# The order of GpSimd's additions and of one VectorE subtraction in an eight-element decoder kernel

## The chip, the cores and the metric

The kernel runs on one core of a Trainium2 chip. The metric is the time of one execution on the device, in microseconds. A core has five engines with a queue each, worked off in order: TensorE (PE in the profile; PEld is its weight load), VectorE (DVE), ScalarE (ACT), GpSimd (POOL) and SyncE (SP, which issues the DMAs). They meet only through semaphores.

## The reference, cut to what matters

Two decoder layers over `x` (8 elements of 256 tokens, 128 features) and a context (8 x 512 x 128). The change lies in layer 0, in the stretch where local self-attention of one element runs beside the cross-attention of the element before it:

```python
x = _layernorm(x + _L0_attn_ref(x, ...))          # 16 heads of 8, causal, window 64, relative bias
x = _layernorm(x + _L0_xattn_ref(x, ctx_1024, ...))
# cross-attention: lat = layer_norm(x)*g+b, ctx = layer_norm(context)*g+b
#   q = lat @ Wq;  k, v = split(ctx @ Wkv);  k = apply_rope(k, cos, sin)      16 heads of 64
#   attn = softmax(clip(q k^T / 8, -11, 11));  out = (attn @ v) @ Wo + bo
x = _layernorm(x + _L0_ffn_ref(x, ...))
x = _layernorm(x + _L1_attn_ref(x, ...))          # a scan of 256 steps
x = _layernorm(x + _L1_xattn_ref(x, ctx_1024, ctx_1024, ...))   # linear attention: relu features
x = _layernorm(x + _L1_ffn_ref(x, ...))
```

## The kernel before, in words

The first 50 us prepare weights and the first element. Then comes a loop over the eight elements `b`, and in it over eight **pairs** of heads `p` of the cross-attention (`batch` on each engine). Behind it follow the scan over 256 steps and the last products (from about 822 us on).

*One pair.* TensorE makes the scores in two halves, the units 0 and 1 (L2133; it waits for `kr_ready`, the rotated keys, and for the exponentials of the unit before). ScalarE takes the exponentials of a unit (L1007, `exps`). VectorE clamps them (L1471, `clamp`), which gives four key blocks `prob[.., 0..3, ..]` of 128 x 512. GpSimd adds the four blocks for the softmax's denominator: first to second (L731, behind the first clamp), plus the third (L733, behind the second clamp), plus the fourth (L735, "the last addition", which signals `psum_ready`). One pair later TensorE multiplies the probabilities by the values (L2057, `values_of`) and the added blocks by ones (L2065, `sum_of`, the column sums, which wait for `psum_ready`). VectorE takes the reciprocal (L1373) and multiplies (L1374, `on`). Keys two pairs ahead are prepared beside this: TensorE's split products (L1758 to L1760, "keys a" and "keys b"), VectorE's multiplications by cosine and sine (L1315, L1317), GpSimd's addition of the two (L641, `rotate`, signals `kr_ready`).

*The slots.* The self-attention of element b+1, with the norms and the layer-1 keys and values of its context, is cut into 48 slots, six to a pair, and each engine calls `self_attention(b + 1, 6 * p + i, ..)` at fixed places among the work of the pair. The order on each engine is written out by hand; there is no planner. The last element has no such slots. Slots named below:
- `S_CTX` = 3 (pair 0): VectorE takes the statistics of the context `cb` (L1176, L1179), GpSimd makes scale and bias of them (`scale_and_bias`, L633 to L636). ScalarE applies them at slot 5 (`apply_norm`, L843).
- `S_CN` = 7 (pair 1): TensorE transposes the normed context; ScalarE copies it with gain and bias twice, as `cn_raw` in full precision (L835) and as `cn_s[.., 0, ..]`, the high part (L906); VectorE subtracts the two into `cn_s[.., 1, ..]`, the low part (L1305, signals `cn_split`). The split products need both. `cn_raw` shares its memory with `ctx_t`, which ScalarE writes in slot 14 behind `cn_split`.
- `S_SCORE` = 6, 8, 10, 12, ...: TensorE makes self-attention scores (L1774), VectorE adds the bias and takes row maxima (L1251, L1253); the next scores go to the same two banks, and wait for that.
- `S_AFFINE` = 36, 38 (pair 6): GpSimd multiplies the layer-1 keys by a gain and adds a bias (L678). VectorE's ReLU of them is slot 40 (L1264), and TensorE's product for them slot 44.
- `S_X1` = 37 (pair 6): GpSimd's norm factor (L624, L626) and an addition.

At pair 0 of elements 1 to 7 TensorE also makes the output product of the element before (`output`, L2040; it waits for `on` of pair 7). VectorE adds it (L1380), takes statistics, waits for GpSimd's factor (L624, L626, behind the rotation in its queue), and normalizes (L1190).

Where GpSimd's additions stand among its slots (L726 to L742): slots 0 and 1 come first, then L731 and L733, then slots 2 and 3, then L735, then slot 4, the rotation, at pair 0 the output's factor, then slot 5. Only two slots with work for GpSimd lie at 2 or 3 of a pair: `S_CTX` in pair 0 and the second of `S_AFFINE` in pair 6. VectorE's order in a pair (L1482 to L1499): keys a, first clamp, slots 0 and 1, reciprocal and product of the pair before, second clamp, slot 2, keys b, slots 3 and 4, the output, slot 5.

Of the kernel before, what the change touches and what calls it, by code (L numbers as in the profile page):

```python
# [57 lines left out]
PER_PAIR = 6  # L58
SLOTS = PER_PAIR * PAIRS
S_X, S_K, S_Q, S_CTX, S_V = range(5)  # L60
S_CN = 7
S_MASKED = (3, 4, 5, 6)
S_SCORE = (6, 8, 10, 12, 14, 16, 18, 20)
S_EXP = (range(10, 14), range(14, 19), range(19, 24), range(24, 29))
# [93 lines left out]
def n(b, per, k):  # L158

    return b * per + k  # L160


class Chain:
# [5 lines left out]
    def link(self, instruction):  # L169
        self.k += 1  # L170
        instruction.then_inc(self.sem, 1)
        self.eng.wait_ge(self.sem, self.k)
# [7 lines left out]
def decoder(nc, a, out):  # L180
    with ExitStack() as ctx:
# [412 lines left out]
        def _(pool):  # L594
# [25 lines left out]
            def rstd_of(before, k, count, eps, half=0, ready=var_ready, done=rstd_ready):  # L620

                tiles = slice(4 * half, 4 * half + count)
                pool.wait_ge(ready, before + k + 1)
                link(g.tensor_tensor(var_eps[:, tiles], mv[:, tiles, 1],  # L624
                                     epsilons[:, EPSILONS.index(eps), tiles], ALU.add))
                g.tensor_tensor(rstd[:, tiles], var_eps[:, tiles], minus_half[:, tiles],  # L626
                                ALU.pow).then_inc(done, 1)
# [10 lines left out]
            def rotate(key):  # L638

                pool.wait_ge(p_free["dve"], KEYS_DONE[key])  # L640
                g.tensor_tensor(kr[:, key % 2, :], k_cos[:, :], k_sin[:, :], ALU.add).then_inc(kr_ready, 1)  # L641
# [72 lines left out]
            def rstd_of_f(b):  # L714
                rstd_of(0, b, QT, 1e-3, half=1, ready=f_var, done=f_rstd)

            def batch(b, last=False):

                for p in range(PAIRS):
                    pair = n(b, PAIRS, p)  # L720

                    def slots(lo, hi):
                        for i in range(lo, hi if not last else lo):
                            self_attention(b + 1, PER_PAIR * p + i, SELF_NORMS * (b + 1))

                    slots(0, 2)  # L726
                    pool.wait_ge(clamped, 2 * pair + 1)
                    if pair >= 2:
                        pool.wait_ge(o_full, pair - 1)
                    pp = prob[:, p % 2]  # L730
                    link(g.tensor_tensor(psum[:, p % 2, :], pp[:, 0, :], pp[:, 1, :], ALU.add))  # L731
                    pool.wait_ge(clamped, 2 * pair + 2)
                    link(g.tensor_tensor(psum[:, p % 2, :], psum[:, p % 2, :], pp[:, 2, :], ALU.add))  # L733
                    slots(2, 4)
                    g.tensor_tensor(psum[:, p % 2, :], psum[:, p % 2, :], pp[:, 3, :],  # L735
                                    ALU.add).then_inc(psum_ready, 1)
                    slots(4, 5)
                    if p + 2 < PAIRS or not last:
                        rotate(pair + 2)
                    if p == 0 and b >= 1:  # L740
                        rstd_of(b - 1, 0, QT, EPS_LN, ready=y_var_ready, done=y_rstd_ready)
                    slots(5, 6)  # L742
                    if last and p < B - 1:
                        rstd_of_f(p)

            for b in range(0, B - 1):
                batch(b)
            batch(B - 1, last=True)
            g.tensor_copy(ident16[:, :], ident[:, :]).then_inc(ident16_ready, 1)
            pool.wait_ge(p_free["dve"], ALL_JOBS["dve"])  # L750
# [75 lines left out]
        def _(act):  # L826
# [45 lines left out]
            def self_attention(b, slot, norms):  # L872
# [26 lines left out]
                if slot == S_LAT:  # L899
                    by_feature = dict(scale=cols[:, LAT_G:LAT_G + 1], bias=cols[:, LAT_B:LAT_B + 1])  # L900
                    evacuate(b, A_LAT, lat_raw[:, :], bank_a[:, 0:T], free=False, **by_feature)
                    s.activation(lat_s[:, b % 2, 0, :], bank_a[:, 0:T], ACT.Identity, **by_feature).then_inc(a_free, 1)
                if slot == S_CN:
                    by_feature = dict(scale=cols[:, CTX_G:CTX_G + 1], bias=cols[:, CTX_B:CTX_B + 1])
# [222 lines left out]
        def _(dve):  # L1127
# [97 lines left out]
            def self_attention(b, slot, norms):  # L1225
# [69 lines left out]
                if slot == S_LAT:  # L1295
                    dve.wait_ge(a_free, n(b, ACT_JOBS, SETUP_A + A_LAT + 1) if b >= 1 else FIRST_LAT)
                    w.tensor_tensor(lat_s[:, b % 2, 1, :], lat_raw[:, :], lat_s[:, b % 2, 0, :].bitcast(F32),
                                    ALU.subtract).then_inc(lat_split, 1)
                if slot == S_CN:
                    if b == 0:  # L1300
                        dve.wait_ge(cn_kept, 1)
                    else:
                        dve.wait_ge(a_free, n(b, ACT_JOBS, SETUP_A + A_CN + 1))
                    raw = cn_raw if b >= 1 else cn_raw_first
                    w.tensor_tensor(cn_s[:, b % 2, 1, :], raw[:, :], cn_s[:, b % 2, 0, :].bitcast(F32),  # L1305
                                    ALU.subtract).then_inc(cn_split, 1)
# [12 lines left out]
            def odd_turn(at):  # L1319
                dve.wait_ge(odd_full, at // 2 + 1)  # L1320
                w.tensor_copy(pt[:, 1, :], ob[:, :]).then_inc(odd_free, 1)

            def first_score(at):
                if at % 2 == 0:
                    dve.wait_ge(bias_in[at // 2], 16)
                self_attention(0, S_SCORE[at], 0)
# [4 lines left out]
            for slot in (S_CTX, S_Q, S_V):  # L1331
                self_attention(0, slot, 0)
# [11 lines left out]
            odd_turn(3)  # L1344
            measure_kv(0, 1)
            odd_turn(5)
            self_attention(0, S_CN, 0)
            odd_turn(7)
            odd_turn(9)
            invert_sums(0)  # L1350
# [398 lines left out]
        def _(pe):  # L1749
# [52 lines left out]
            def self_attention(b, slot):  # L1802
                def a_job(job):
                    pe.wait_ge(a_free, n(b, ACT_JOBS, SETUP_A + job))
# [85 lines left out]
                if slot == S_LAT:  # L1890
# [4 lines left out]
                    last.then_inc(a_full, 1)  # L1895
                if slot == S_CN:
                    a_job(A_CN)
# [557 lines left out]
```

## Time and profile before

| | us |
|---|---|
| median of 3 runs | 1050.55 |
| the three runs | 1050.55, 1050.72, 1046.6 |
| the profiled execution, its own time | 1047.62 |
| its span, first to last instruction | 1045.9 |
| TensorE busy | 919.8 (88%) |
| VectorE busy | 681.3 (65%) |
| GpSimd busy | 510.7 (49%) |
| ScalarE busy | 509.6 (49%) |
| mean granted clock of TensorE, share of full speed | 0.944 |

In the rows further down a timeline gives for each instruction (or group of the same) its start in us from the start of the span, its duration in us, engine, line, operation, output and inputs with partitions x elements, and how many; in brackets how long the engine had been idle before, and which engine's work ended that idle time. An instruction's bracket is missing where the engine was not idle. Starts can lie up to 0.1 us ahead of the end of the instruction before, since an engine overlaps the two. A row of the chain gives start, duration and what the chain passed through. A clock of 1.00 is 2.4 GHz, and the low level is 1.2 GHz.

### The profile page before, as it was taken

Reading aid. Unit: us, or ns where it says so; the run is one execution under the profiler, and the core shown is the slowest. Engines: PE = TensorE matmul, PEld = TensorE weight load, DVE = VectorE, ACT = ScalarE, POOL = GpSimd, SP = SyncE. Lnnn points to the kernel's source line nnn. Section 1 sums busy time; section 2 is a strip of 40 time slices with the busy share of each in tenths; the row PEclk is TensorE's granted clock in tenths of the full one; section 3 lists DMA queues with packets and bytes.
Section 4 is the critical chain, followed back from the end, with each engine's and each line's share of the span. In section 5 each row is a group of like instructions: output and inputs, shape, how many; then the busy total and the mean of one; then the engine's idle time right before and its main releaser. Section 6 shows DMA issues by size and latency. Waiting matters only on the chain.

```text
span 1045.9 us, 22097 instructions
## 1 busy us (share of the span) xinstructions
PE 919.8 (88%) x8504; PEld 652.6 (62%) x8504; DVE 681.3 (65%) x1906; ACT 509.6 (49%) x1441; POOL 510.7 (49%) x642
## 2 busy tenths in 40 slices
PE   6689989998999999899989999998988499999922
PEld 4456656666665756566666666666656379888721
DVE  6446577568757766776687577667689543444477
ACT  6655645653663556456636645564233023333324
POOL 2643475356546534654565466446657112333363
PEclk9989999999999989999999999999999589999955
DMA  7000000000000000000000000000000001222211
GB/s 194 21 6 12 1 2 6 12 1 7 11 1 1 7 11 2 1 6 11 2 6 7 6 1 1 1 1 1 21 1 1 0 7 30 32 33 30 33 13 41
DMA packets 60470, 15.09 MB, mean 14 GB/s; under 512 B 41278, under 2 KB 59726, under 8 KB 60238
## 3 DMA queue, kind: packets, MB, share of 16 engines
q1 hardware_dynamic: 60366, 13.69, 6.1%
q8 instruction: 68, 1.11, 0.4%
q14 instruction: 36, 0.29, 0.1%
HBM read 10.51 MB, written 3.17 MB: 13 GB/s over the span
## 4 chain that ended last, share of the span: by engine, by line
PE 64%; DVE 19%; ACT 7%; POOL 5%; issue 3%; DMA 1%; SPq 0%; POOLq 0%; DVEq 0%; ACTq 0%
PE score_banks L2133 10%; PE out_bank L2057 8%; PE score_banks L1758 5%; DVE o_rec L1373 5%; PE bank_a L1753 5%; PE score_banks L2071 4%; DVE prob L1471 3%; PE score_banks L1789 3%; PE score_banks L1760 3%; PE score_banks L1759 3%; PE score_banks L2261 3%; PE bank_d L1774 3%; PE out_bank L2040 2%; PE out_bank L2065 2%; PE bank_d L2274 2%
## 5 line engine op out<-in xcount | busy, mean ns | idle before, releaser
L1007 ACT ACTIVATE prob<-score_banks 128x1024 f32<-128x1024 f32 x128 | 131.0, 1024 | 165.8 <-PE score_banks L2133 165.5
L733 POOL TENSOR_TENSOR psum<-psum,prob 128x512 f32<-128x512 f32 x64 | 81.6, 1275 | 153.9 <-DVE prob L1471 153.9
L2133 PE MATMUL score_banks<-qh,kr 64*128 64x256 f32 x1024 | 150.9, 415 | 2.1 <-ACT qh L916 1.3
L731 POOL TENSOR_TENSOR psum<-prob 128x512 f32<-128x512 f32 x64 | 82.6, 1290 | 98.4 <-DVE prob L1471 98.3
L1373 DVE RECIPROCAL o_rec<-out_bank 128x256 f32<-128x256 f32 x64 | 111.9, 1748 | 26.1 <-PE out_bank L2065 26.0
L2057 PE MATMUL out_bank<-prob,v 128*64 128x256 f32 x1024 | 124.7, 386 | 1.4 <-DVE on L1374 1.4
L2133 PEld LDWEIGHTS score_banks<-qh,kr 64*128 64x128 f32 x1024 | 91.9, 193 | 40.7 <-issue 30.5
L867 ACT ACTIVATE prob<-prob,neg_max 128x128 f32<-128x128 f32 (+1 forms) x256 | 107.1, 426 | 13.5 <-DVE neg_max L1258 13.5
L1471 DVE TENSOR_SCALAR prob<-prob 128x1024 f32<-128x1024 f32 x128 | 101.4, 792 | 12.9 <-ACT prob L1007 12.9
L2057 PEld LDWEIGHTS out_bank<-prob,v 128*64 128x64 f32 x1024 | 67.9, 136 | 46.6 <-issue 17.2
L1056 ACT ACTIVATE prob<-score_banks 128x8 f32<-128x8 f32 x255 | 45.1, 177 | 96.1 <-PE score_banks L2261 96.1
L1315 DVE TENSOR_TENSOR k_cos<-score_banks,cos_t 128x512 f32<-128x512 f32 x56 | 38.2, 682 | 72.4 <-PE score_banks L1760 46.2
L641 POOL TENSOR_TENSOR kr<-k_cos,k_sin 128x512 f32<-128x512 f32 x64 | 82.8, 1294 | 4.4 <-DVE k_sin L1317 3.6
L735 POOL TENSOR_TENSOR psum<-psum,prob 128x512 f32<-128x512 f32 x64 | 81.6, 1275 | 3.9
L2261 PE MATMUL score_banks<-prob,pt 128*64 128x8 f32 x1020 | 74.3, 210 | 0.6 <-ACT prob L1053 0.3
L835 ACT ACTIVATE pt<-bank_a 128x512 f32<-128x512 f32 x84 | 50.2, 598 | 35.5 <-PE bank_a L1753 34.6
L1774 PE MATMUL bank_d<-km,q 64*128 64x128 f32 x480 | 50.6, 330 | 17.9 <-DVE row_max L1253 16.6
L2261 PEld LDWEIGHTS score_banks<-prob,pt 128*64 128x64 f32 x1020 | 53.4, 137 | 20.8 <-ACT prob L1056 14.5
L2071 PE MATMUL score_banks<-w_qkv_t,ident 128*64 128x96 f32 (+1 forms) x336 | 64.8, 277 | 0.0
L1753 PE MATMUL bank_a<-ident,prob 128*128 128x128 f32 x360 | 57.0, 281 | 4.0 <-ACT pt L835 2.3
L1789 PE MATMUL score_banks<-pt,vm 128*32 128x128 f32 x768 | 54.0, 281 | 4.5 <-ACT pt L938 3.8
L760 POOL TENSOR_TENSOR var_eps<-mv,epsilons 128x1 f32<-128x1 f32 x49 | 9.5, 194 | 96.1 <-DVE mv L1575 96.1
(414 smaller groups left out, 2129.8 us busy)
## 6 DMA issues: line engine op xcount, KB each, us to landing
cb<-in_ctx_dram SPq DMA_DIRECT2D x8, 256.0 KB, 2.8
bias_mask<-bias_scratch SPq DMA_DIRECT2D x4, 384.0 KB, 5.4
xb<-in_x_dram SPq DMA_DIRECT2D x8, 128.0 KB, 2.1
prob<-in_L_xattn_Wkv_dram SPq DMA_DIRECT2D x1, 1024.0 KB, 8.4
x_scratch<-v SPq DMA_DIRECT2D x16, 64.0 KB, 1.5
bias_mask<-x_scratch SPq DMA_DIRECT2D x16, 64.0 KB
att_scratch<-on SPq DMA_DIRECT2D x16, 64.0 KB, 1.5
prob<-att_scratch SPq DMA_DIRECT2D x16, 64.0 KB, 3.0
```

The costliest lines, as they stand in the source:

```text
L641: g.tensor_tensor(kr[:, key % 2, :], k_cos[:, :], k_sin[:, :], ALU.add).then_inc(kr_ready, 1)
L731: link(g.tensor_tensor(psum[:, p % 2, :], pp[:, 0, :], pp[:, 1, :], ALU.add))
L867: last = s.activation(pr, pr, ACT.Exp, bias=neg_max[:, qt, j, g:g + 1], accum_out=row_sum[:, qt, j, g:g + 1])
L1007: s.activation(prob[:, p % 2, 2 * u:2 * u + 2, :].rearrange("p k (h q) -> p h k q", h=2), sc[:, 0:2, :].rearrange("p h (k q) -> p h k q", ...
L1373: link(w.reciprocal(o_rec[:, :], bank[:, T:2 * T]))
L1471: w.tensor_scalar(pr, pr, float(np.exp(-CLIP)), float(np.exp(CLIP)), ALU.max, ALU.min).then_inc(clamped, 1)
L1753: return nc.tensor.transpose(out_ap, in_ap, ident[0:in_ap.shape[0], 0:in_ap.shape[0]])
L1789: last = mm(o0_bank[32 * g:32 * g + 32, qt * P:(qt + 1) * P], vm[:, kt, j, 32 * g:32 * g + 32], pt[:, t % 2, i * P:(i + 1) * P], start=(j ...
L2057: mm(o[DH * h:DH * (h + 1), 0:T], v[:, (q // 2) % 2, kb, lo:lo + DH], prob[:, q % 2, kb, T * h:T * (h + 1)], start=(kb == 0), stop=(kb == ...
L2071: mm(bank[0:HALF_ROWS, 0:columns], ident[:, 0:HALF_ROWS], w_qkv_t[:, 0:columns], start=True, stop=True, skip_group_check=True)
L2133: last = mm(sc[:, h, k * T:(k + 1) * T], kr[rows_of, p % 2, kb * P:(kb + 1) * P], qh[rows_of, p % 2, :], start=True, stop=True, skip_group ...
L2261: last = mm(cf[lo:lo + HALF_ROWS, t * B:(t + 1) * B], a_t[:, lo:lo + HALF_ROWS], hid[:, (t - 1) * B:t * B], start=False, stop=True, skip_g ...
```

## The change

The slot of VectorE's low part gets a number of its own, 11 instead of 7: it moves from pair 1's slot 1 (ahead of the reciprocal of pair 0) to pair 1's slot 5 (behind the self-attention scores of slots 8 and 10). TensorE's and ScalarE's part of `S_CN` stays at 7. On GpSimd the slots 2 and 3 of a pair go behind the last addition; with slot 4 they make one call. The call for element 0 follows the new name and stays where it is.

```diff
-S_CN = 7
+S_CN, S_CN_LOW = 7, 11
...
                     link(g.tensor_tensor(psum[:, p % 2, :], psum[:, p % 2, :], pp[:, 2, :], ALU.add))
-                    slots(2, 4)
                     g.tensor_tensor(psum[:, p % 2, :], psum[:, p % 2, :], pp[:, 3, :],
                                     ALU.add).then_inc(psum_ready, 1)
-                    slots(4, 5)
+                    slots(2, 5)
                     if p + 2 < PAIRS or not last:
                         rotate(pair + 2)
...
-                if slot == S_CN:
+                if slot == S_CN_LOW:
                     if b == 0:
                         dve.wait_ge(cn_kept, 1)
...
-            self_attention(0, S_CN, 0)
+            self_attention(0, S_CN_LOW, 0)
```

## Rows read from the trace of the kernel before

**Rows 1.** The page's first part: busy us, share of the span, instructions.
```profile
PE 919.8 (88%) x8504; PEld 652.6 (62%) x8504; DVE 681.3 (65%) x1906; ACT 509.6 (49%) x1441; POOL 510.7 (49%) x642
```
**Rows 2.** Waits of TensorE, 60 to 825 us: total, times, longest.
```profile
PE out_bank L2065 <- POOL psum L735: 16.7, 7, 2.4
PE bank_d L1774 <- DVE row_max L1253: 14.8, 7, 2.4
```
**Rows 3.** The chain of waits, in two stretches.
```profile
243.80 0.65 PE out_bank L2065 x4
...
269.05 0.03 DVE cn_s L1305
```
**Rows 4.** Windows between low parts: us, PE busy, granted clock, DMA share, GB/s.
```profile
172.54:269.05 96.51, 90.75 (x691) 0.98 0.02 5
269.05:364.23 95.18, 89.27 (x691) 1.00 0.02 5
```
**Rows 5.** Timeline of GpSimd, pair 6 of element 1.
```profile
241.27 1.26 POOL L678 TENSOR_TENSOR k<-k,l_b 128x512 f32<-128x512 f32 x1
242.49 1.26 POOL L735 TENSOR_TENSOR psum<-psum,prob 128x512 f32<-128x512 f32 x1
243.71 1.45 POOL L641 TENSOR_TENSOR kr<-k_cos,k_sin 128x512 f32<-128x512 f32 x1
```
**Rows 6.** Timeline of VectorE, pairs 6, 7 and 0.
```profile
242.56 1.47 DVE L1264 TENSOR_SCALAR k<-k 128x512 f32<-128x512 f32 x1 [0.69 <-POOL k L678]
245.26 0.69 DVE L1315 TENSOR_TENSOR k_cos<-score_banks,cos_t 128x512 f32<-128x512 f32 x1 [1.23 <-POOL kr L641]
...
256.72 0.42 DVE L1374 TENSOR_TENSOR on<-out_bank,o_rec 128x256 f32<-128x256 f32 x1
```
**Rows 7.** Timeline of TensorE, the output product in pair 0 of element 2.
```profile
258.18 3.74 PE L2040 MATMUL out_bank<-wo,on 128*128 128x128 f32 x32
```
**Rows 8.** Timeline of GpSimd, pair 0 of element 2.
```profile
258.17 1.27 POOL L733 TENSOR_TENSOR psum<-psum,prob 128x512 f32<-128x512 f32 x1 [1.80 <-DVE prob L1471]
260.29 0.20 POOL L633 TENSOR_TENSOR var_eps<-mv,epsilons 128x4 f32<-128x4 f32 x1 [0.85 <-DVE mv L1179]
...
262.09 1.27 POOL L735 TENSOR_TENSOR psum<-psum,prob 128x512 f32<-128x512 f32 x1
...
264.83 0.71 POOL L626 TENSOR_TENSOR rstd<-var_eps,minus_half 128x2 f32<-128x2 f32 x1
```
**Rows 9.** Timeline of VectorE, pairs 0 to 2 of element 2.
```profile
262.03 0.42 DVE L1380 TENSOR_TENSOR y<-out_bank,x 128x256 f32<-128x256 f32 x1 [0.71 <-PE out_bank L2040]
...
265.58 0.60 DVE L1190 TENSOR_SCALAR x<-y,mv,rstd 128x128 f32<-128x128 f32 x2 [2.32 <-POOL rstd L626]
...
267.02 0.69 DVE L1471 TENSOR_SCALAR prob<-prob 128x1024 f32<-128x1024 f32 x1
...
269.05 0.69 DVE L1305 TENSOR_TENSOR cn_s<-ctx_t,cn_s 128x512 fp32r<-128x512 f32 x1 [0.36 <-ACT cn_s L906]
...
277.53 0.69 DVE L1315 TENSOR_TENSOR k_cos<-score_banks,cos_t 128x512 f32<-128x512 f32 x1 [2.01 <-PE score_banks L1760]
```
**Rows 10.** Timeline of ScalarE, first exponentials of pair 1, element 2.
```profile
264.53 1.00 ACT L1007 ACTIVATE prob<-score_banks 128x1024 f32<-128x1024 f32 x1
```
**Rows 11.** Timelines of VectorE and GpSimd in pair 7: a subtraction beside an addition.
```profile
246.47 0.42 DVE L1297 TENSOR_TENSOR lat_s<-x_t,lat_s 128x256 fp32r<-128x256 f32 x1
...
246.63 1.39 POOL L731 TENSOR_TENSOR psum<-prob 128x512 f32<-128x512 f32 x1 [1.47 <-DVE prob L1471]
```
**Rows 12.** Element 0: GpSimd's scale and bias, VectorE's low part and next instruction.
```profile
68.39 0.20 POOL L633 TENSOR_TENSOR var_eps<-mv,epsilons 128x4 f32<-128x4 f32 x1 [1.21 <-DVE mv L1179]
...
75.79 0.69 DVE L1305 TENSOR_TENSOR cn_s<-ctx_t,cn_s 128x512 fp32r<-128x512 f32 x1 [0.46 <-ACT cn_s L906]
76.40 1.75 DVE L1373 RECIPROCAL o_rec<-out_bank 128x256 f32<-128x256 f32 x1
```
**Rows 13.** Timeline of VectorE, pair 0 of element 7.
```profile
737.48 1.76 DVE L1373 RECIPROCAL o_rec<-out_bank 128x256 f32<-128x256 f32 x1 [0.83 <-PE out_bank L2065]
```

## The prediction

> **What bounds the kernel now.** First the page's busy times: TensorE is busy for 919.8 of 1045.9 us, no other engine for more than 681.3 [rows 1]. So time can only go where TensorE stands still, or where it is slow. Next the waits of TensorE while the eight batch elements are worked on: two causes come first, each once per element that has a successor. Seven waits of 2.4 us are for GpSimd's last addition of a pair, seven of about 2.1 us for VectorE's score step [rows 2]. Then the chain of waits: it runs through both places. At 243.80 it goes on with TensorE's column sums, behind GpSimd; at 269.05 it passes through VectorE's low part of the context [rows 3]. The change touches these places and nothing else. From one low part to the next an element takes 95.18 us at a granted clock of 1.00 [rows 4].
>
> I work through one turn, from pair 6 of element 1 (239 us) to pair 2 of element 2 (278 us). The others repeat it.
>
> **Part 1, pair 6: the last addition ahead of the affine step.** GpSimd now runs L678 (1.26 us), then L735, then the rotation L641 [rows 5]. With the two exchanged, L735 starts at 241.27 and ends at about 242.55, 1.22 us earlier than its 243.75. TensorE waits for just this, so its column sums, the transposes of the latents and unit 1 of pair 7 move up by 1.22 us. L678 ends where L735 ended, and the rotation starts where it did, so the next keys get nothing. What is late instead is VectorE's L1264 (ReLU of the keys), which waits for L678: from 242.56 to about 243.85. Before, it overlapped an addition of GpSimd and took 1.47 us; now it overlaps the rotation [rows 5, 6]. If the two exclude each other as they did, L1264 ends near 245.3, when the waiting multiplication by the cosine starts anyway (245.26). I charge 0.06 us. The bounds: a gain of 0.18 us (the rotation's 1.45 against the 1.27 of the additions of the same size [rows 8]) and a loss of 1.2 us (L1264 begins its 1.47 us only behind the rotation). I take the value near zero because the row of the same pair shows just this overlap, resolved in that order.
>
> How much of the 1.22 us lives on? The output product of element 0 starts on TensorE at 258.18 [rows 7], and needs VectorE's product of pair 7, which ends at 256.72 + 0.42 = 257.14 [rows 6]. That one hangs on the rotation at 243.71 and on GpSimd's three jobs of pair 7, none of which gets earlier. So the output starts at about 257.3: 0.9 us of the 1.22 are left.
>
> **Part 2, pair 0: the last addition ahead of the context's scale and bias.** GpSimd ends its third addend at 259.44, stands idle for 0.85 us until VectorE's statistics of the context are there, works 1.8 us on scale and bias, and only then adds (262.09), rotates behind that, and finds the output's factor (L626, ends 265.54) [rows 8]. VectorE waits 2.32 us for that factor [rows 9]. With the addition moved up it starts at about 259.5 and ends at 260.8. Scale and bias start then, 0.46 us later than now; the rotation and the factor come 1.27 - 0.46 = 0.8 us earlier. Part 1 gives another 0.1 to 0.2 us, since VectorE's second clamp no longer waits for ScalarE. The factor's other input, the statistics of the output, moves up with the output product: VectorE's addition at 262.03 waits 0.71 us for TensorE, and can go 0.7 to 0.9 us earlier. I take 0.9 us for the start of L1190 (265.58), with 0.7 as the low end.
>
> What is late now: ScalarE's normalization of the context, by 0.3 to 0.46 us, and behind it on that in-order queue the first exponentials of pair 1. They end at 265.53 [rows 10], and would end at 266.0 at the latest. The clamp that reads them starts at 267.02 [rows 9] and would start at 266.1: just covered. In element 0 this cover is thinner, see below. The column sums of pair 0 are not waited for here, so the addition itself gives nothing.
>
> **Part 3, pair 1: the low part four slots later.** At 269.05 VectorE waits 0.36 us for ScalarE's copy and subtracts for 0.69 us, ahead of the reciprocal of pair 0, the second clamp, and the score step that TensorE waits some 2.1 us for (14.8 us in seven times) [rows 2, 9]. Taken out, it gives 0.36 + 0.60 = 0.96 us (the next instruction starts 0.60 us behind it, as in [rows 12]). It comes back behind the scores of slot 10, where VectorE has 2.01 us of idle time until the product of the keys (277.53) [rows 9]. TensorE and VectorE both move up, so this cover stays, and I cost it at nothing; without it 0.69 us. Its readers are far off: ScalarE's copy of the transposed context, in pair 2 slot 14, and the keys of pair 6.
>
> The row nearest to the low part in its new place, beside a rotation, is L1297, the same kind of subtraction with both inputs in SBUF: 0.42 us beside an addition that took 1.39 instead of some 1.27 us [rows 11]. So the price would be 0.1 us, on GpSimd, which nobody waits for there. The Trainium skill, GPSIMD Engine Reference, section Key points, says that GpSimd shares its SBUF interfaces with VectorE and contends with VectorE instructions that have two SBUF inputs or run in a 2-port mode. If VectorE were the one to wait, the low part would take up to 0.69 + 1.27 = 1.96 us, which would use up its cover; L1297's row speaks against it, while L1264's 1.47 us agrees for the other kind.
>
> **Sum of a turn:** 0.9 (parts 1 and 2 overlap; they meet at L1190) + 0.96 = 1.86 us, below the 2.1 us that TensorE stands at the score step plus what it gained already. From there to pair 6 of the next element TensorE, ScalarE and VectorE hang on each other and nothing on a fixed time, so it is kept.
>
> **Over the elements.** Elements 1 to 6: 6 x 1.86 = 11.2 us. Element 0 has no output before it. There the addition fits the idle 1.21 us ahead of scale and bias; ScalarE, through which its chain runs, comes 0.1 us later; the low part (0.46 us wait, 0.60 us work [rows 12]) goes. Together 1.06 - 0.12 = 0.9 us. Element 7 has no slots for a next one, but inherits part 1: its reciprocal at 737.48 waits 0.83 us for the sums [rows 13], so 0.85 us. Total 11.2 + 0.9 + 0.85 = 12.9, say 13 us.
>
> The profiled execution took 1047.62 us (span 1045.9 and 1.7 around it); less 13 that is 1034.6. The median of the runs shown is 1050.55, 2.9 us above, and one run is at 1046.6; less 13 the median gives 1037.5. The profiled run lies at the low end of three that differ by 4 us, so I forecast between the two: **1036 us**.
>
> **The rivals.**
> - *Only the low part pays* (chance 0.12). L1190's wait isn't shortened, because the factor's statistics, not GpSimd's queue, come last, and part 1 is eaten before the output. Then 7 x 0.9 = 6.3 us, 1043 from the middle. For it: the cover of 0.85 us and the idle 0.71 us are rough. Against it: VectorE's wait of 2.32 us begins long before GpSimd starts L624.
> - *The shared memory path takes it back* (0.10). L1264 is held for the whole rotation and then runs its 1.47 us, at pair 7. Keys, clamp and everything up to the output are 1.2 us later, and a turn gives 1.86 - 1.2 = 0.66 us: about 5 us in all, 1044. For it: VectorE's 1.47 us beside GpSimd. Against it: the rotation's own 1.45 us shows that the two take turns within one instruction.
> - *Slower by the clock* (0.05). TensorE's granted clock is 1.00 in most elements and 0.98 in one that took 96.51 us: one stretch at 1.2 instead of 2.4 GHz costs about 1.3 us [rows 4]. The waits are moved to other places and the pattern of such stretches may change for the worse. It decides from ten more of them on; with two more in each of seven elements, +18 - 13 = +5 us, 1054. Against it: TensorE's standstills become shorter, none longer.
> - *More than forecast* (0.13): all 1.22 us of part 1 and 0.96 us survive, and a stretch at the low clock goes: 7 x 2.2 + 1.3 = 17 us, 1032.
>
> **How the numbers follow.** The forecast case has 0.60; its own range is 1034 to 1039, by the two bases and some 1.5 us of rounding. For 8 in 10 I reach from 1031.5 (the last rival) to 1043 (the first). Half a per cent, about what a measurement of this kernel can tell from no change, is 5.2 us. Faster by more than that: the forecast, the last rival, most of the first, part of the second: 0.86. Within: 0.10. Slower: 0.04.
>
> **What would show it.** Right: TensorE's seven waits of 2.4 us at L2065 shrink to about 1.2 us; those at the score step to about 1.1 us; VectorE's wait ahead of L1190 is below 2.3 us and L1190 itself starts some 0.9 us earlier in the turn; the low part sits in front of an idle stretch; the turn is 93.3 instead of 95.2 us. Wrong: the cosine product of pair 7 begins clearly later behind L1264; the first exponentials of pair 1 hold up the clamp or unit 1; or the turn is shorter and the sum is not, because stretches at the low clock came in.

## The result, and the profile after

The changed kernel takes 1025.66 us (median of 4 runs, 1023.58 to 1026.37) against 1049.22 us for the one before (4 runs, 1046.6 to 1050.72): a ratio of 0.9776, 95% interval 0.9753 to 0.9799, or 23.6 us less. The forecast was 1036 us in a range of 1031.5 to 1043: the sign was right, the size not. The profiled execution took 1023.58 us, its span 1021.9 against 1045.9 us.

The busy times of the changed kernel, from the page, to be held against [rows 1]:

```profile
PE 910.6 (89%) x8504; PEld 646.2 (63%) x8504; DVE 685.5 (67%) x1906; ACT 509.7 (50%) x1441; POOL 510.2 (50%) x642
```

The work is the same, instruction for instruction, and yet TensorE is busy for 9.2 us less and VectorE for 4.2 us more. Both have a cause further down: TensorE ran less of its time at the low clock, and VectorE's moved subtraction became slower.

TensorE's waits of the changed kernel, 55 to 810 us (to [rows 2]; what waits, for whom, total us, times, longest):

```profile
PE out_bank L2064 <- POOL psum L734: 8.1, 7, 1.2
PE bank_d L1773 <- DVE row_max L1252: 6.4, 7, 1.2
```

The column sums wait for 1.2 us each, as forecast, and the score step for 0.9 us on average (forecast about 1.1). Lines behind L735 have moved up by one: L2065 is L2064 here, L1305 is L1304.

Where the time went: one turn from the first addition of pair 4 to that of the next element, windows of TensorE (stretch, its length, TensorE busy, granted clock, DMA share, GB/s). First the kernel before:

```profile
117.17:213.70 96.53, 90.77 (x692) 0.98 0.02 5
213.70:308.88 95.18, 89.27 (x692) 1.00 0.02 5
308.88:406.84 97.96, 92.20 (x692) 0.97 0.02 5
406.84:503.56 96.72, 90.82 (x692) 0.98 0.02 5
503.56:598.75 95.19, 89.28 (x692) 1.00 0.02 5
598.75:695.24 96.49, 90.74 (x692) 0.98 0.01 1
```

and the first and the last of the six turns of the changed kernel; the four between read 93.01 to 93.04 us at 1.00:

```profile
112.87:205.87 93.00, 89.54 (x692) 1.00 0.02 6
...
577.98:671.02 93.04, 89.56 (x692) 1.00 0.00 1
```

A turn at full clock has gone from 95.18 to 93.03 us: 2.15 us, six times 12.9 us. Beyond that, the six turns of before hold 578.07 - 6 x 95.18 = 7.0 us that belong to stretches at the low clock, and the changed kernel has none there. These two make 19.9 of the span's 24.0 us. Another 4.3 us are gained up to pair 4 of element 0. Of them 1.7 us lie in the preparation, which the change does not touch: the kernel before happened to have two low stretches there in its profiled execution, the changed one a single one. That part is luck. The rest, 2.6 us, comes from one low stretch of some 1.5 us less and the low part's move. Behind the six turns 0.2 us are lost again: 1.1 us are gained up to a wait of TensorE of 1.16 us for the keys, late in element 7, and 1.3 us are lost behind it, where the low stretch is 6.8 us long instead of 3.4.

### The profile page after: what moved, and what is told of

Same layout as the page of the kernel before. It is cut to its first block, busy times and chain, and to the rows that moved or that the text cites. A ratio compares the mean times of both kernels' runs of the same rounds, so it can differ in the third digit from the quotient of the medians.

```text
span 1021.9 us, 22090 instructions
## 1 busy us (share of the span) xinstructions
PE 910.6 (89%) x8504; PEld 646.2 (63%) x8504; DVE 685.5 (67%) x1906; ACT 509.7 (50%) x1441; POOL 510.2 (50%) x642
## 4 chain that ended last, share of the span: by engine, by line
PE 51%; DVE 26%; POOL 11%; ACT 6%; issue 4%; DMA 1%; SPq 0%; POOLq 0%; DVEq 0%; ACTq 0%
PE score_banks L2132 7%; DVE o_rec L1372 7%; PE out_bank L2056 6%; DVE prob L1470 6%; PE bank_a L1752 4%; PE score_banks L2070 4%; PE score_banks L1757 4%; PE score_banks L1788 3%; PE score_banks L2260 3%; POOL psum L733 3%; POOL psum L734 2%; PE bank_d L2273 2%; PE bank_d L1773 2%; PE score_banks L1758 2%; PE score_banks L1759 2%
## 5 line engine op out<-in xcount | busy, mean ns | idle before, releaser
L2132 PE MATMUL score_banks<-qh,kr 64*128 64x256 f32 x1024 | 146.2, 404 | 2.2 <-ACT qh L915 1.3
L2132 PEld LDWEIGHTS score_banks<-qh,kr 64*128 64x128 f32 x1024 | 89.1, 187 | 39.7 <-issue 30.0
```

The source lines that it names most:

```text
L2132: last = mm(sc[:, h, k * T:(k + 1) * T], kr[rows_of, p % 2, kb * P:(kb + 1) * P], qh[rows_of, p % 2, :], start=True, stop=True, skip_group ...
```

## The experiments

All runs are compared with runs of the kernel before on the same chip; "turn" is the quantity above.

**GpSimd's move in pair 0 alone.**

```diff
+                    ahead = 2 if p == 0 else 4
-                    slots(2, 4)
+                    slots(2, ahead)
                     g.tensor_tensor(psum[:, p % 2, :], psum[:, p % 2, :], pp[:, 3, :],
                                     ALU.add).then_inc(psum_ready, 1)
-                    slots(4, 5)
+                    slots(ahead, 5)
```

> GpSimd's last addition moved ahead in pair 0 only (context's scale and bias behind it); pair 6 and the low part as before. Theory: VectorE gets the output's factor earlier by GpSimd's queue, but the output product starts as before, so the output's statistics come no earlier; 0.3 to 0.8 us a turn, 1042 to 1048 us. Rival: the whole gain of GpSimd's part (1.05 us a turn) comes from pair 0; then it equals the kernel with GpSimd's part alone.

Measured: 1047.07 us, ratio 1.0004 (0.9976 to 1.0032), no gain, where 0.3 to 0.8 us a turn were expected. A turn without a low stretch is as long as before:

```profile
601.45:696.62 95.17, 89.28 (x692) 1.00 0.01 1
```

The distance from pair 0 to pair 1 does shrink by 0.8 us, but VectorE's timeline shows where it goes (the row to hold against 269.05 in [rows 9]):

```profile
267.35 0.69 DVE L1306 TENSOR_TENSOR cn_s<-ctx_t,cn_s 128x512 fp32r<-128x512 f32 x1 [1.14 <-ACT cn_s L907]
```

The low part now waits 1.14 instead of 0.36 us for ScalarE's high part, which hangs on TensorE's transposes and so on the output. The 0.8 us turn into a wait.

**GpSimd's two moves without VectorE's.** The GpSimd hunk of the change, alone.

> The kernel before with GpSimd's part of the change alone; the low part stays at slot 7. Theory A (two parts of about 1.05 us a turn each, and standstills of TensorE over 2 us that are followed by stretches at the low clock): the turn at full clock is 94.1 instead of 95.2 us, TensorE still stands 2.1 us at the score step but only 1.2 us at the column sums of pair 6, and some of the low stretches stay: 1036 to 1042 us. Theory B (the extra 10 us over the forecast have to do with the order itself, not the clock): the turn at full clock is shorter by 2 us or more already. Rival C (GpSimd's order alone is covered by the low part): 1048 to 1050 us.

Measured: 1042.3 us, just above the expected range, ratio 0.9956 (0.9933 to 0.9979), 4 to 5 us less.

**VectorE's move without GpSimd's.** The other hunks.

> The kernel before with VectorE's low part at slot 11 and GpSimd's order unchanged. Theory A: turn at full clock 94.1 us, standstill at the score step about 1.1 us, the 2.4 us at the column sums stay with the stretches that follow them: 1036 to 1042 us. The low part takes 1.6 us beside the rotation and nobody waits. Rival: its 1.6 us are on the path, then less than 0.3 us a turn are gained, 1047 us or more.

Measured: 1040.91 us, ratio 0.9936 (0.9909 to 0.9963). One gives 0.44%, the other 0.64%, both together 2.24%: about twice the sum. The third turn of each shows why, windows of TensorE, first GpSimd's moves alone, then VectorE's:

```profile
309.43:405.19 95.76, 91.06 (x692) 0.98 0.02 5
```
```profile
307.68:403.38 95.70, 90.87 (x692) 0.98 0.02 5
```

In either kernel no turn is at a clock of 1.00; each holds one low stretch. Each kernel also keeps one of the two standstills of TensorE: some 2.1 us, seven times, at the score step in the one, and 2.4 us, seven times, at the column sums in the other. The low stretch follows that standstill in both. In the kernel before, with windows cut at the standstill:

```profile
362.00:366.70 4.70, 4.70 (x34) 1.00 0.02 3
366.70:368.77 2.07, 0.00 (x0) 0.97 0.00 0
368.77:375.60 6.83, 6.83 (x29) 0.51 0.00 0
375.60:380.00 4.40, 4.40 (x40) 1.00 0.00 0
```

in the kernel with VectorE's move alone, at the column sums:

```profile
622.50:624.87 2.37, 0.00 (x1) 1.00 0.00 0
624.87:625.96 1.09, 1.09 (x8) 1.00 0.00 0
625.96:629.37 3.41, 3.41 (x15) 0.50 0.00 0
629.37:635.00 5.63, 5.30 (x36) 1.00 0.00 0
```

and in the one with GpSimd's moves alone, at the score step:

```profile
174.72:176.80 2.08, 0.00 (x1) 1.00 0.00 0
176.80:178.72 1.92, 1.77 (x16) 1.00 0.00 0
178.72:182.13 3.41, 3.41 (x12) 0.50 0.03 5
```

TensorE works at 1.00, stands for 2.1 or 2.4 us, and then a stretch of 3.4 or 6.8 us goes at 0.5, that is 1.2 GHz. In these three kernels it begins between 0.3 us before and 1.9 us behind the end of the standstill. In the kernel before, 6 of 14 such standstills are followed by a low stretch, with GpSimd's move in pair 0 alone 5 of 14; in either half kernel all seven that it keeps are. Which one is hit the rows don't say. It seems to differ between executions: 33 runs of the kernel before on one chip range from 1040.48 to 1052.73 us, and their spans go with the mean granted clock, from 1038.8 us at 0.950 to 1051.0 us at 0.941.

**The clock by itself.** The order of the kernel before, and idle matmuls, whose results nothing reads, in front of the two waits:

```diff
             def sum_of(pair):
                 q = pair % PAIRS
+                if q == PAIRS - 2 and pair < (B - 1) * PAIRS:
+                    for _ in range(8):
+                        mm(ob[0:DH, T:2 * T], ident[:, 0:DH], w_qkv_t[:, 0:T], start=True, stop=True, ...)
...
                     pe.wait_ge(km_ready, n(b, H // 2, at + 1))
+                    if at == 2:
+                        a_job(A_CN + 1)
+                        for _ in range(7):
+                            mm(bank_a[0:DH, 0:T], ident[:, 0:DH], w_qkv_t[:, 0:T], start=True, stop=True, ...)
```

> The kernel before in its old order, with idle matmuls of TensorE put into its two long standstills (8 ahead of the column sums of pair 6, 7 ahead of the score step of slot 10), whose results nothing reads. Theory A: the order and all waits of the others stay, the turn at full clock stays 95.2 us, but the low stretches of the element loop go, and with them 7 to 10 us: 1039 to 1043 us. Rival: the low stretches come of themselves and not from the standstills; then the time stays at 1047 to 1050 us or grows by what the idle matmuls cost.

Measured: 1050.28 us, ratio 1.0029 (1.0001 to 1.0057). It missed, and is not conclusive by its time: all low stretches in the turns are gone, but a turn is 96.8 us, because the matmuls were too many. At the score step they took 3.2 us for a wait of 2.1 us. So the same with 5 and 4:

> The kernel before with fewer idle matmuls: 5 ahead of the column sums of pair 6 and 4 ahead of the score step, some 2.3 and 1.9 us, so that they end inside the standstills of 2.4 and 2.1 us. Theory A (the standstills bring the low stretches): all turns are 95.2 us at full clock, no low stretch in elements 1 to 6, and the time is 1039 to 1042 us with nothing else changed. Rival (the low stretches had nothing to do with the standstills, and their absence with more filling was chance): 1047 to 1050 us.

Measured: 1038.21 us, ratio 0.9893 (0.9876 to 0.991), 10.6 us less with none of the kernel's own work moved. The first turn, from the windows (the others read 95.16 or 95.17 us at 1.00):

```profile
116.55:211.72 95.17, 93.29 (x710) 1.00 0.02 5
```

The length at full clock is the old one, so what the filling gives comes through the clock. The profiled spans differ by 9.6 us, and 7.1 of them lie in the six turns; the changed kernel gains the same 7.0 us there. With the low stretch of element 0 some 8.5 of the measured 23.6 us are what the two standstills above 2 us cost through the clock, and TensorE's busy time, 9.2 us less for the same work, agrees. (Another 1.9 us of the filled kernel lie behind the turns, where the changed kernel gains nothing.) The same filling, 5 matmuls at the column sums only, in the kernel with VectorE's move alone:

> The kernel with the low part's move alone, and 5 idle matmuls in the standstill of 2.4 us at the column sums that it still has. Its own trace showed one low stretch a turn (turn 95.7 us). Theory A: with the filling the low stretches go and the turn is 94.2 us, 7 x 1.5 = 10 us less than the same kernel unfilled: 1030 to 1032 us. Rival: the low stretches stay, 1039 to 1041 us.

Measured: 1030.72 us, ratio 0.9845 (0.9813 to 0.9878), and

```profile
206.78:300.91 94.13, 91.43 (x702) 1.00 0.02 5
```

against 95.70 us unfilled. The low part's move gives 95.18 - 94.12 = 1.06 us a turn, and the low stretch behind the standstill that it keeps takes 95.70 - 94.12 = 1.6 us.

**The change without its part in pair 0** (`p == 6` in the first diff, and the low part's move).

> The changed kernel without its part in pair 0: the last addition moved ahead in pair 6 only, and the low part at slot 11. Theory: the earlier factor is of use only if both pair 6 brings the output forward and GpSimd's queue in pair 0 is shorter; then this kernel loses some 0.5 to 0.9 us a turn against the changed one (turn 93.5 to 93.9 us), 1029 to 1032 us if no standstill above 2 us comes back. Rival: pair 0 is worth nothing here too (as it was alone), then it is level with the changed kernel, 1024 to 1027 us.

Measured: 1029.64 us, ratio 0.9811 (0.9793 to 0.983); five of six turns at 93.79 us. Pair 6 is worth 94.12 - 93.79 = 0.33 us on top of the low part, and pair 0 another 93.79 - 93.03 = 0.76 us on top of both, though nothing alone. One turn of this kernel, 95.32 us, holds a low stretch:

```profile
358.53:359.79 1.26, 0.00 (x1) 1.00 0.00 0
359.79:361.86 2.07, 1.93 (x16) 1.00 0.00 0
361.86:365.27 3.41, 3.41 (x13) 0.50 0.00 0
```

The standstill ahead of it took only 1.26 us, so a short one is no safe one. In the turns of the changed kernel none is followed by a low stretch.

**The low part's new place.** In the changed kernel it takes more than twice its old time, beside GpSimd's rotation. VectorE and then GpSimd in the changed kernel:

```profile
265.42 1.58 DVE L1304 TENSOR_TENSOR cn_s<-ctx_t,cn_s 128x512 fp32r<-128x512 f32 x1
267.52 0.69 DVE L1314 TENSOR_TENSOR k_cos<-score_banks,cos_t 128x512 f32<-128x512 f32 x1 [0.52 <-PE score_banks L1759]
```
```profile
265.19 1.27 POOL L641 TENSOR_TENSOR kr<-k_cos,k_sin 128x512 f32<-128x512 f32 x1
```

GpSimd started first, ran to 266.46, and VectorE finished 0.54 us later. I put it two slots further up, `S_CN_LOW = 9`:

> The changed kernel with the low part at slot 9 instead of 11, directly behind the keys' product with the sine: beside the last addition of the pair, with no idle time behind it but the score step that TensorE waits for. If the low part's 1.58 us in the changed kernel is turn-taking with GpSimd's rotation that only idle time hides, it is 1.1 to 1.9 us here as well and delays TensorE's score steps: 0.5 to 1.5 us a turn lost, 1028 to 1036 us. Rival: it takes 0.7 us beside an addition, and the turn stays within 0.3 us: 1024 to 1028 us.

Measured: ratio 0.9774 (0.9753 to 0.9796), level with the changed kernel (the rival of the expectation); the turn is 93.00 us. There the low part takes 1.36 us beside the last addition, and the rotation behind it 1.73 instead of 1.27 us. The turn-taking is as expected, but my guess that it would cost time there was wrong: VectorE still stands idle for 0.76 us behind the scores of that pair.

**Two attempts at a faster kernel.** In the changed kernel VectorE's second clamp of pair 6 meets GpSimd's first addition, which started at 230.11:

```profile
230.37 1.57 DVE L1470 TENSOR_SCALAR prob<-prob 128x1024 f32<-128x1024 f32 x1
231.86 1.57 DVE L1189 TENSOR_SCALAR lat<-x,mv,rstd 128x128 f32<-128x128 f32 x2
```

First, in the changed kernel, GpSimd's first addition of pair 6 ahead of slot 37 (`slots(0, 1)`, the addition, `slots(1, 2)`):

> The changed kernel, and in pair 6 GpSimd's first addition ahead of the slot with its norm factor (slot 37), in a stretch where it stands idle for 2 us. VectorE's second clamp of pair 6 then no longer meets that addition and takes 0.7 instead of 1.6 us. Expected: third and last addition, column sums and keys 0.8 us earlier a turn, 1019 to 1022 us. Rival: the clamp now meets another GpSimd job, or the norm factor comes late by the addition, and nothing is won: 1025 us.

Measured: ratio 0.9779 (0.9754 to 0.9804), nothing, where 4 to 7 us were expected. Second, also the output's factor ahead of the rotation in pair 0:

> As the last one, and in pair 0 GpSimd's factor for the output ahead of the rotation. VectorE waits 2.2 us for that factor and needs the rotation only one instruction later. Expected: another 0.4 to 0.6 us a turn over the last one, 1015 to 1020 us. Rival: the factor's statistics come late and hold the rotation, level with the last one or slower.

Measured: ratio 0.9771 (0.9754 to 0.9788), nothing that the time can tell, where some 3 us more were expected; the turn is 92.91 us, 0.1 us less. VectorE in pair 6 of the first, and in pair 0 of the second:

```profile
231.29 1.56 DVE L1191 TENSOR_SCALAR x<-y,mv,rstd 128x128 f32<-128x128 f32 x2
...
235.67 0.68 DVE L1472 TENSOR_SCALAR prob<-prob 128x1024 f32<-128x1024 f32 x1
```
```profile
257.83 1.55 DVE L1191 TENSOR_SCALAR x<-y,mv,rstd 128x128 f32<-128x128 f32 x2 [1.09 <-POOL rstd L626]
```

In pair 6 the clamp is fast now, 0.68 us, and the normalization of y, which was 0.59 us, pays for it with 1.56 us: the moved addition meets that one instead. In pair 0 VectorE's wait for the factor falls from 2.17 to 1.09 us, and its normalization rises from 0.60 to 1.55 us beside the rotation. In both places the gain is spent on the neighbour.

**Clear of each other.** So GpSimd's jobs must lie beside VectorE work that does not take turns with them: the statistics, and the reciprocal, which reads PSUM. Two moves on the changed kernel, first the addition behind VectorE's normalized x, then also the affine step ahead of pair 5's last slot:

```diff
-                    slots(0, 2)
+                    inner = p == PAIRS - 2 and not last
+                    if not inner:
+                        slots(0, 2)
                     pool.wait_ge(clamped, 2 * pair + 1)
+                    if inner:
+                        pool.wait_ge(x1_ready, b + 2)
...
                     link(g.tensor_tensor(psum[:, p % 2, :], pp[:, 0, :], pp[:, 1, :], ALU.add))
+                    if inner:
+                        slots(1, 2)
...
+                    if p == PAIRS - 3:
+                        slots(6, 7)
                     slots(5, 6)
```

The addition's move alone has `slots(0, 1 if inner else 2)` and no `slots(6, 7)`.

> As the last one with the first addition's move alone; the affine step still meets the first clamp of pair 6. Expected: second clamp 0.7 us, normalization 0.6 us, 0.9 us earlier: 1019 to 1022 us. Rival: 1025 us.

Measured: 1018.87 us, ratio 0.9714 (0.969 to 0.9738), turn 92.42 us; the second clamp takes 1.00 us, the normalization of y 0.59. Both moves:

> The changed kernel with two GpSimd jobs moved to where VectorE runs nothing that the last runs showed to take turns with them: the first affine step of the keys ahead of the factor at the end of pair 5, and the first addition of pair 6 behind a wait for VectorE's normalized x (x1_ready), beside its statistics and reciprocal. Expected: VectorE's first and second clamp of pair 6 and its normalization all at full speed (0.7, 0.7, 0.6 us instead of 1.5, 1.6, 0.6), last addition 1.5 to 1.8 us earlier, TensorE's standstill at the column sums gone, 0.8 to 1.2 us a turn: 1016 to 1020 us. Rival: the jobs meet other instructions again, as in the last two runs: 1025 us.

Measured: **1014.1 us**, ratio 0.967 (0.9649 to 0.9691), turn 91.65 us, faster than both kernels. VectorE and GpSimd in pair 6:

```profile
224.90 0.69 DVE L1478 TENSOR_SCALAR prob<-prob 128x1024 f32<-128x1024 f32 x1
225.66 0.60 DVE L1197 TENSOR_SCALAR x<-y,mv,rstd 128x128 f32<-128x128 f32 x2
...
226.98 1.72 DVE L1380 RECIPROCAL o_rec<-out_bank 128x256 f32<-128x256 f32 x1
...
229.08 0.89 DVE L1478 TENSOR_SCALAR prob<-prob 128x1024 f32<-128x1024 f32 x1
```
```profile
222.85 1.28 POOL L678 TENSOR_TENSOR k<-k,l_g 128x512 f32<-128x512 f32 x1
...
226.39 1.27 POOL L735 TENSOR_TENSOR psum<-prob 128x512 f32<-128x512 f32 x1 [0.77 <-DVE prob L1478]
```

Both clamps and the normalization of y run at or near full speed (0.69, 0.89 and 0.60 us, where the changed kernel has 1.52, 1.57 and 0.59), and TensorE's wait at the column sums is gone from the head of its list.

## Why the prediction was wrong in size

- **Part 1, pair 6: right.** The last addition moved up by 1.2 us against the first of that pair, TensorE's wait fell from 2.4 to 1.2 us. The ReLU behind the affine step took 1.47 us beside the rotation, and the next cosine product came no later, as charged. Of the 1.22 us I let 0.9 survive to the output product; counted from the first addition of pair 6, it starts at 19.18 instead of 20.24 us, so 1.06 survived.
- **Part 2, pair 0: right in kind.** L1190 was forecast 0.9 us earlier, and is 1.12 (26.52 instead of 27.64 us behind the same mark). Its wait is 2.17 instead of 2.32 us. ScalarE's exponentials end at 257.81, VectorE's clamp starts at 258.07: the cover held by 0.26 us. That this part is worth nothing alone I had not said; it follows from the 0.36 us wait for ScalarE that I had read and counted only as a gain.
- **Part 3, the low part: the gain right, its price wrong.** 0.96 us forecast, 1.06 measured. I priced it in its new place by L1297 in [rows 11], which had started 0.16 us *ahead* of its neighbour, so that GpSimd paid. The low part starts behind it, and VectorE pays 0.9 us. The Trainium skill, GPSIMD Engine Reference, section Key points, names an instruction with two SBUF inputs as one that contends with GpSimd; the trace agrees at 1.58 against 0.69 us. I had named this case as the bound, up to 1.96 us, and set it aside for a row that spoke only of who came first. The idle time of 2.0 us covered it, with 0.52 us left.
- **The sum of a turn** came to 1.86 us; it was 2.15. Over the elements that mis-sizes the forecast by 2 us.
- **The step that failed is the clock.** The sum of a turn has no term for the low stretches. I gave them to a rival on the slow side ("the pattern of such stretches may change for the worse"), and one of them to the rival "more than forecast". The runs show a gain of some 8.5 us in its place: 7.0 us in the six turns, where all low stretches go, and 1.5 us in element 0. In the kernel before they follow standstills of 2.1 to 2.4 us, which the change cuts to 1.2 us and less, and filling these standstills alone takes them out of the turns as well. The evidence was in the trace of before. I wrote that the clock is "1.00 in most elements" and 0.98 in one, from the two windows of [rows 4]; that reading is wrong, since four of the six turns are below 1.00. I had the price of a stretch, 1.3 us, and did not cut windows at the waits. With 7 us for the turns, 1.5 us for element 0 and the 2 us above the forecast would have been 1025.5 us, beside 1025.66 measured; that these lie so close is in part luck, as the preparation and element 7 show.
- **What stays open** is why a given standstill is followed by a low stretch and another is not. One of 1.26 us was hit in the kernel without the part in pair 0, and one of 1.16 us in element 7 of the changed kernel, so the change makes low stretches rare in the turns and does not rule them out.

## What to carry to other kernels

Cut the windows of the granted clock at TensorE's waits before pricing them: a standstill of 2.1 to 2.4 us cost its own length and, where a low stretch followed, 1.3 to 1.6 us more (2.8 to 3.0 us where the stretch was 6.8 us long). Two edits that each remove one standstill of two were together worth twice their sum here. A GpSimd addition slowed VectorE's subtraction, clamp and normalization within SBUF when it ran beside them, and not its statistics or its reads of PSUM, so place it beside the latter, and look at the neighbour that a moved job meets as well as at the one it leaves.

## What the runs showed of the hardware that was not expected

The granted clock fell to 1.2 GHz for 3.4 or 6.8 us around the end of single standstills of 2.1 to 2.4 us (from 0.3 us before it to 1.9 us behind it), although TensorE was busy almost without a gap before and behind them. The Trainium skill, TensorE: Matmul & The Clock Gate, section What's actually happening, says that activity releases the throttle; the run with 5 and 4 idle matmuls agrees, with no low stretch in six turns where the kernel before has four turns with one.

VectorE's subtraction of 128x512 with both inputs in SBUF took 0.69 us alone, 1.58 us when GpSimd's addition of the same size had started 0.23 us before, and 1.36 us at 0.47 us behind it. Where VectorE came first, GpSimd's rotation took 1.73 instead of 1.27 us. The reciprocal from PSUM took 1.72 to 1.76 us whatever GpSimd did, and the statistics of 128x128 took 0.27 to 0.30 us, beside one of its additions or not.
